# AdaLN transformer layer on one core: new order of the steps, 95 score units on row tiles, ten more unread products

## What is computed

```python
mod = (_silu(L0_c) @ L0_wmod).reshape(4, 6, 1, -1)          # sa, ca, ga, sb, cb, gb; |ga|, |gb| at least 0.25
h = _layernorm(x) * (1 + ca) + sa
x = x + ga * attention(h)      # 16 query heads summed in groups onto 4 key heads, d = 16, rope, causal softmax over 1024
h = _layernorm(x) * (1 + cb) + sb
x = x + gb * ffn(h)            # per position: h if not routed, else h' + mlp(rmsnorm(h')),
                               # h' = h + (rmsnorm(h) @ wv) @ wo, mlp = silu(a @ w_gate) * (a @ w_up) @ w_down, 704 wide
```

## Time and profile before

| | |
|---|---|
| median of 3 runs | 460.96 us |
| the profiled execution: its own time | 461.26 us |
| its span, first to last instruction | 459.5 us |
| mean granted TensorE clock | 0.996 of full |
| TensorE busy (matmuls) | 431.0 us, 94% |
| VectorE busy | 350.9 us, 76% |
| ScalarE busy | 307.9 us, 67% |
| POOL busy | 190.8 us, 42% |
| chain that ended last, by engine | TensorE 81%, VectorE 7%, ScalarE 5% |

### The profile page before, as it was taken

How to read it: one execution, slowest core, us unless ns; L and a number is a source line. 1 busy time by engine, 2 the same in 40 slices (tenths; PEclk the granted TensorE clock), 3 DMA queues, 4 the chain that set the end, 5 groups by cost and what they waited for, 6 DMA issues and landing times.

```text
span 459.5 us, 9532 instructions
## 1 busy us (share of the span) xinstructions
PE 431.0 (94%) x3320; PEld 364.0 (79%) x3320; DVE 350.9 (76%) x796; ACT 307.9 (67%) x640; POOL 190.8 (42%) x308
## 2 busy tenths in 40 slices
PE   6897879888999999999999999999999999999996
PEld 6575444776586688997858999999898698999996
DVE  4789958789988578998847889888975755588554
ACT  2398588775688886527697645667768698646441
POOL 6485546410256210424917204533244333436633
PEclk9998999999999999999999999999999999999999
DMA  6940030000001000020120000000010000000001
GB/s 192 324 152 14 1 100 0 2 1 3 0 3 34 22 1 1 2 69 1 44 71 24 2 1 24 1 26 24 2 58 3 24 23 3 25 1 24 23 25 47
DMA packets 16577, 16.05 MB, mean 35 GB/s; under 512 B 4233, under 2 KB 14926, under 8 KB 16530
## 3 DMA queue, kind: packets, MB, share of 16 engines
q1 hardware_dynamic: 16530, 15.44, 10.9%
HBM read 11.09 MB, written 4.21 MB: 33 GB/s over the span
## 4 chain that ended last, share of the span: by engine, by line
PE 81%; DVE 7%; ACT 5%; issue 3%; POOL 1%; DMA 1%; SPq 1%; ACTq 0%; DVEq 0%; POOLq 0%
PE banks L812 9%; PE banks L814 9%; PE banks L813 9%; PE banks L740 6%; PE banks L703 6%; PE banks L599 6%; PE banks L601 6%; PE banks L600 6%; PE banks L728 6%; PE banks L681 5%; DVE mxp L1185 2%; PE banks L691 2%; ACT xTc L913 1%; PE banks L795 1%; PE banks L776 1%
## 5 line engine op out<-in xcount | busy, mean ns | idle before, releaser
L812 PE MATMUL banks<-gTh,guhi 128*128 128x256 f32 x352 | 101.4, 288 | 0.1
L814 PE MATMUL banks<-gTh,gulo 128*128 128x256 f32 x352 | 98.9, 281 | 0.0
L813 PE MATMUL banks<-gTl,guhi 128*128 128x256 f32 x352 | 98.8, 281 | 0.0
L957 ACT ACTIVATE PT<-banks 128x1024 f32<-128x1024 f32 (+3 forms) x96 | 74.3, 813 | 27.7 <-PE banks L728 22.5
L812 PEld LDWEIGHTS banks<-gTh,guhi 128*128 128x128 f32 x352 | 66.4, 189 | 1.9 <-issue 1.1
L1185 DVE TENSOR_REDUCE mxp<-banks 128x2 f32<-128x1024 f32 (+3 forms) x56 | 62.1, 1142 | 6.6 <-PE banks L703 3.9
L813 PEld LDWEIGHTS banks<-gTl,guhi 128*128 128x128 f32 x352 | 66.5, 189 | 0.3
L814 PEld LDWEIGHTS banks<-gTh,gulo 128*128 128x128 f32 x352 | 66.3, 188 | 0.0
L703 PE MATMUL banks<-QKT 128*128 128x512 f32 (+3 forms) x192 | 50.3, 371 | 7.0 <-ACT QKT L935 3.4
L599 PE MATMUL banks<-wdhi,ffhi 128*128 128x256 f32 x160 | 46.1, 288 | 0.0
L728 PE MATMUL banks<-QKT 64*128 64x512 f32 (+7 forms) x192 | 44.1, 382 | 1.2 <-ACT PT L957 0.9
(11 more groups left out here) (180 smaller groups left out, 1101.0 us busy)
## 6 DMA issues: line engine op xcount, KB each, us to landing
xres<-in_L_attn_x SPq DMA_DIRECT2D x8, 512.0 KB, 4.2
out_x<-xres SPq DMA_DIRECT2D x16, 256.0 KB, 2.1
...
modB<-mod_scratch SPq DMA_DIRECT2D x4, 256.0 KB, 3.4
...
```

The source lines that it names most:

```text
L812: pe.matmul(out_, guhi[:, k, blk, :], gh, start=(m == 0 and k == 0), stop=False)
L813: pe.matmul(out_, guhi[:, k, blk, :], gl, start=False, stop=False)
L814: i = pe.matmul(out_, gulo[:, k, blk, :], gh, start=False, stop=(m == len(blocks) - 1 and k == KB - 1))
L957: act.activation(PT[:, u % 2, 2 * q:2 * q + 2, 0:CH - q0], both("prob", b, n)[:, :, 0:CH - q0], ACT.Exp, scale=float(D) ** -0.5).then_inc( ...
```

## The change

`ORDER` is replaced as a whole. It has 1450 words again, the same number of each kind; their sequence, the banks and the marks differ. Marked are now 72 `prob` and 23 `max` steps. `FILL` is keyed by batch too, and puts 3 unread products ahead of the first `max` of batch 0, 2 ahead of its first `yT`, and 5 ahead of its first `ynT`, beside the 6 ahead of the first `qkv`. In `max`, `yT` and `ynT` the wait for the bank now comes ahead of the wait for the data, with the unread products between.

The diff, with most of the two lists left out:

```diff
--- before.py
+++ after.py
@@ -42,7 +42,7 @@
 NX = 3
 WARM, WIDE = 14, CH // (2 * KB * B)
 
-FILL = {('qkv', 0): 6}
+FILL = {('max', 0, 0): 3, ('yT', 0, 0): 2, ('ynT', 0, 0): 5, ('qkv', 0, 0): 6}
 HALVES = slice(0, CH // 2), slice(CH // 2, CH)
 
 
@@ -111,65 +111,65 @@
 
 
 ORDER = """
-ldx ldx ldx ldx pzero asetw stats setw pmodc vmodc rstd1 norm1 norm1 xT4 xev qkv5 stats norm1 norm1 xT4 xev qkv4 asetb
-setb pmod amod rstd1 norm1 norm1 xT6 xev norm1 norm1 xT7 qkvb qkvb rope pprep0 afwv vkeys sthi qkv6 xev aprep pprep1
-aw1 gmod stlo qkvb qkv7 qkvb gprep stats rstd1 norm1 stack4 stack6 rope stk max4 max0 stk mxr mxr sthi stlo aprep max6
-max2 max4 stack0 mxr stack6 stk aprep mxr mxr max2 max0 max4 mxr stk mxr max2 max0 mneg mtT6 mrow max6 mxr mxr mxr ldW
-ldB ldG ldG max2 max0 max4 mxr mxr mxr max6 mxr mxr mrd prob2' aprep awd exp norm1 gprep max0 max4 prob6' max2 mxr mxr
-exp prob0' max6 prob4' exp norm1 norm1 gprep gw1 gprep gwd pmask max0 exp mxr mxr mxr pv2 prob4' prob6' pmask pv
-prob0' exp exp pmask exp prob4' exp mneg mtT3 mrow mrd ldx pmask pv pv ycopy yT2 xT3 xev xT4 wob woh ldx stats ytm
-ynT5 ynev prob2 prob0 rstd1 wol norm1 wo5 x1 rstd2 norm1 norm1 norm2 exp exp norm1 prob6' exp prob2' prob0' pv5 prob6
-exp wo2 pv exp exp prob0' exp x1 rstd2 prob6' exp stats rstd1 pv prob2' prob0' prob6' exp exp pv exp hT2 hhi prob0
...
-ytm a3 route stlo h2 h2T2 a5 qkv7 h2hi ynT3 qkvb qkvb stack0 ms2 ynev stk stack6 h2lo stk route ms2 max0 rope sthi
-max4 max6 up2 mxr mxr max0 norm1 rs2 norm1 h2 gate3 sil max4 mxr max6 mxr stlo mxr mxr stack0 stack4 stk h2 max0 fft
-max2 h2T6 stk mneg mtT7 mrow h2hi mxr mxr max4 max0 max2 norm1 mxr mxr mxr max4 wo7 max0 h2lo mxr max2 gate6 ffhi sil
-mrd prob4 x1 rstd2 exp wo6 gate7 mxr mxr max0 mxr prob4' prob2' x1 exp exp max0 mxr max4 prob2 pmask pv6 norm1 exp
-pmask mxr max0 mxr max2 prob4 exp pv prob4 exp woh mxr max0 mxr mneg pmask prob4 exp up2 prob4 exp xT3 xev norm1 norm1
-pmask rstd2 norm2 gate0 fflo fft sil pv pv mtT3 mrow norm2 sil hT1 hhi hlo ycopy ms1 rs1 up4 xT2 norm1 ffhi gate3 yT6
...
+ldx stats asetw setw rstd1 pmodc norm1 norm1 norm1 xT5 norm1 vmodc xev qkv5 stats xT7 xev vkeys rstd1 asetb pmod pzero
+norm1 setb qkv7 amod norm1 qkvb norm1 xT4 norm1 qkvb pprep0 gmod xev rope xT7 afwv qkv4 pprep1 xev qkvb sthi stlo qkv3
+aw1 stats stack4 stack0 qkvb stk rope stk max6 max2 max4 mxr sthi max0 mxr ldW aprep stlo max2 mxr stack6 gprep mxr
+max4 stk mxr stack0 mxr stk max6' mneg max4 mxr mtT1 mrow mxr max6 aprep mrd max0 ldx ldx ldG mxr max2' mxr aprep
+gprep mxr max0 max6 mxr rstd1 prob4' prob2 exp mxr max0' norm1 exp prob4 mxr gw1 max6 exp max2 mxr pmask prob0 exp wob
+max6' mxr aprep pmask mxr gprep max2' max0 awd mxr max4 pv7 mxr woh mxr prob0' prob2' exp pv exp mneg prob0' prob4 exp
+pmask exp mtT6 pmask mrow pv norm1 pv norm1 ycopy mrd ldx gprep yT1 xT6 ytm xev wol ynT4 stats ynev gwd ldW prob0
...
+norm2 exp xT4 pmask prob2 prob0 stats exp a7 rs1 exp prob2 xev prob0' pmask pv route norm1 a4 exp exp ms2 hT2 pmask
+route pv hhi norm1 pv hlo qkv0 ms2 norm1 ms1 qkvb rs2 a3 ycopy qkvb rs1 h2 xT7 rope h2 yT6 xev xT1 h2T5 h2hi qkv2 ytm
+sthi a0 xev route ynT7 ynev qkv4 stlo qkvb ms2 h2lo stack6 qkvb stack2 stk route rope stk max6 max0 mxr sthi max2 mxr
+gate6 stlo max0 mxr sil max4 mxr stack2 mxr max0 stk stack6 mxr wo4 stk max2' mneg mxr mtT5 up0 mrow x1 ms2 mrd max2'
+rs2 gate7 fft rstd1 mxr h2 h2 max4 sil max0 mxr h2T3 mxr max6' h2hi prob4' exp h2lo mxr max2 prob0 mxr max6 exp mxr
+prob2' pmask max4' exp prob0' rstd1 mxr ffhi max6 exp max2 mxr wo4 norm1 pmask max0' mxr gate7 rstd2 x1 norm1 pv6 mxr
+prob2' max4' exp pv mxr woh max0 prob2 mxr max4 exp pmask prob2' mxr exp prob0 norm1 exp up3 rstd2 sil mneg pmask up0
...
 """.split()
@@ -615,7 +615,7 @@
 
                 def fill(kind, n):
                     free(kind, n)
-                    for _ in range(FILL.get((kind, n), 0) if b == 0 else 0):
+                    for _ in range(FILL.get((kind, b, n), 0)):
                         pe.matmul(of(kind, b, n)[:, 0:P], ident[:], ident[:], start=True, stop=True)
 
                 if kind == "pmodc":
@@ -693,8 +693,8 @@
                     i.then_inc(S["stack"], 1)
                 elif kind == "max":
                     qt, k0, kn, at = MAX_UNITS[n]
+                    fill(kind, n)
                     wait("stk", qt // 2 + 1)
-                    free(kind, n)
                     o = both(kind, b, n)
                     diag = k0 + kn == (qt + 1) * P
                     for m, q in enumerate(at):
```

More of the change, by code:

```diff
@@ L139 @@
-sil up1 ffl fft max4 mxr max2 max0 wo6 max4 up7 mxr mxr mxr gate2 x1 sil ffhi fft max4 mxr up3 ffhi fflo max0 mxr
-gate2 sil fft ffl wo7 woh max4 mxr down6 sum prob0 rs1 a2 route x1 prob4 down6 sum ffhi exp exp prob0 prob4 exp rstd2
-pmask rstd2 exp fflo max2 mxr pv7 ms2 prob4' exp prob0' exp a6 max4 route ms2 pmask pmask pv prob0' prob2' exp down6
-rs2 exp pmask pv pv mxr mneg mtT2 store ldx stats sum hT3 h2 h2 h2T4 ycopy yT7 ytm mrow mrd down6 fin rstd1 store
-norm1 ynT7 hhi hlo sum fin store norm1 h2hi h2lo a5 route wol ldW ldx ldG a6 prob2 prob0 prob4 route ynev wo7 x1 norm2
@@ new lines @@
+sil xev prob6' a0 fflo exp yT3 hT4 ytm down1 ms1 route hhi prob6 route ms2 ynT3 exp down2 sum hlo ynev ms2 prob6' sum
+prob0' exp fin prob4' pv3 exp wo6 exp a2 x1 prob0' norm1 pv store exp ldG ldB rs1 prob4' prob6' norm1 exp route pv rs2
+exp prob4' prob0' rstd2 ms2 up2 exp norm1 exp a7 pv pmask route prob4' fft prob0' exp prob6' pv exp wo4 ms2 exp prob0
+rs2 x1 qkv2 h2 h2 pmask h2 up5 exp pmask h2T1 fft xT0 prob6 norm2 xev prob4' pv pv h2hi exp gate0 h2lo exp ffhi pmask
+fflo norm1 up4 sil norm1 pv qkv5 qkvb rstd2 ycopy xT1 qkvb ffhi hT2 xev xT6 fft ffl gate3 rope hhi qkv7 sil ffhi wob
@@ new lines @@
+yT4 xev qkvb up5 fflo sthi gate1 fft stlo ffhi h2 qkv5 hlo sil ytm stack2 qkvb stack0 stk gate4 rope max6 sil up2 ms1
+mxr fflo stk up5 fft max6 fft sthi max2 mxr h2T4 ffhi max0 h2hi mxr ffl max6 down5 mxr mxr stlo ynT1 max6 norm2 stack2
+down0 stk mxr sum ynev h2lo max2' stack6 sum mxr wo4 stk gate5 x1 ffhi max2' mneg sil max6 rstd2 mxr max0 fin mtT5 mxr
+up4 mrow mxr max2 fft max0 mxr store up4 mxr max6' fflo max2' gate5 ldx mrd mxr mxr max0 sil gate6 ffhi fft mxr max2
+sil max4 mxr up7 mxr max2 prob0' mxr exp wo4 down5 fflo x1 ffhi prob0' woh max2 fft down4 exp mxr ffhi pmask sum ffl
@@ new lines @@
+prob0 sum max2 exp fflo prob4' mxr pv7 exp rs1 prob0' mneg prob4' pmask exp a3 exp mtT0 route pmask mrow prob4' pv fin
+stats pv ms1 mrd a2 exp prob0 hT6 exp route down5 ms2 pmask store ms2 hhi rs2 prob2' sum prob0' exp pv rstd1 down5
+ycopy exp rs1 h2 yT7 norm1 h2 sum prob0' hlo norm1 prob2' exp fin ytm prob4' pv6 exp a1 exp prob2' route ynT0 exp h2T4
+a7 h2hi rstd2 ldG store xT5 ynev route pv xev wol prob0' prob2' exp h2lo pv ldW ldx norm2 exp prob4 prob0' exp pv exp
+prob4' prob2' exp hT7 pmask wo1 exp prob4' x1 pv ms2 pmask ms2 prob2' exp rs2 pv stats exp prob0' norm1 prob4' exp up3
@@ new lines @@
+exp pmask h2 hhi rstd1 ms1 gate0 hlo h2 norm1 a2 sil rs1 h2T5 a7 norm1 route pmask qkv1 h2hi norm1 wob ms2 fft pv
+norm2 ffhi pv xT4 up3 xev norm1 route ldB norm1 gate0 qkvb h2lo qkv7 sil ms2 fft ycopy xT0 fflo gate1 xev qkvb rope
+ffhi hT2 sil up6 ffl qkv5 fft sthi wo7 qkvb rs2 up4 hhi stlo hlo rstd2 xT5 x1 gate1 xev ffhi yT6 sil stack2 fflo h2
+qkv7 ytm h2 stk stack0 qkvb down6 stk rope ms1 max2 sthi down0 rs1 mxr sum fft ffhi max4 sum stlo h2T7 fin gate0 mxr
+h2hi max2 sil up4 mxr store h2lo ynT2 fft gate1 norm2 a5 sil fflo gate0 ynev route up7 sil ms2 wo4 fft ffhi stack2 x1
@@ new lines @@
+ffl wo6 stk a0 up5 route ffhi gate4 fft x1 max0 sil stack2 ms1 mxr up4 ms2 rs1 fflo ffhi hT5 fft max6 rstd2 hhi down0
+stk mxr rs2 hlo h2 max6 h2 sum fflo down1 mxr max4' sum max2' mneg fin a1 mxr h2T0 mtT7 mxr gate6 h2hi mrow h2lo max4
+ffhi norm2 mrd sil up7 ffl gate2 route a0 fft ms2 ms1 up3 mxr route sil ffhi up1 fft fflo ffhi ms2 max4' max6' mxr rs2
+gate0 rs1 mxr up4 sil max2 fft gate0 ffhi mxr h2 ffl h2 fflo max6' sil prob2' h2T5 exp fft rstd2 down1 mxr h2hi hT7
+sum ffhi down4 h2lo hhi norm2 prob2' prob0' sum exp up5 hlo fin exp max2' prob0' mxr gate7 exp ms1 pmask fflo max0 sil
@@ new lines @@
+a3 mxr a6 route gate0 fft ms2 route ffhi up7 sil fflo ms2 woh max4 rs2 down2 mxr rstd2 h2 h2 fft rs1 wol max6' sum hT0
+mxr h2T1 pmask max2' h2hi down5 ffhi hhi hlo max6 sum h2lo gate4 fin mxr up5 sil mxr prob2' pv0 fft ldG store store pv
+exp max4 prob6 mxr gate1 exp pmask norm2 prob6 prob4 exp a3 exp ffhi a2 route sil ldB store pmask gate6 ffl mneg up5
+sil ms1 pv fft pv route mtT7 ycopy up5 ffhi fflo mrow yT6 fft hT4 ms2 mrd gate3 ytm hhi ffhi ms2 fflo up2 sil rs2
+down0 fft ffl ffhi h2 rs1 prob2' sum prob6' exp fflo down5 ynT0 sum down1 hlo ynev fin exp a4 h2 sum prob2 route wo5
```

54 lines of the change are left out of this document (15 added, 39 removed).

## The result

| | before | after |
|---|---|---|
| median of 20 runs each, in turn on one chip | 461.77 us | 459.18 us |
| lowest to highest | 460.85 to 466.02 | 455.27 to 461.81 |
| profiled execution: its own time | 461.26 | 459.68 |
| its span | 459.5 | 458.0 |
| its mean granted clock | 0.996 | 0.985 |

The ratio of the times is 0.9925, with a 95% interval of 0.9906 to 0.9944: some 3 us faster, where 458.1 us and a gain of 2.9 us were predicted. The time is in the range. The way to it is not the predicted one, and the rest of this text is about that. Of all runs in this text one (of old_order_new_marks, 474.95 us) fell into a slower state of the chip and is left out of its median and means.

A forecast was written before the change was run, and what follows sets the result against it. TensorE bounds 115 to 440 us; before that VectorE's pace and the waits count. Marks 5.1 us less, changes of form 3.2 more, head 1.0 less: 2.9 less than 461.26, 458.4, set at 458.1 for the median; range 454.0 to 464.0.

The forecast's parts named there:

- Part 1: Behind about 131 us, 43 more marked units on TensorE, 0.14 us saved per unit of 512 columns: 5.1 us less.
- what would show it: List of signs; one: a marked unit between full products has pitch 0.33 to 0.43, products beside it 0.1 more each.
- Part 2: Behind about 131 us, TensorE switches between full array, marked units and `pv` 101 times instead of 52: 3.2 us more.
- R to C: nothing: On TensorE, going from marked units (two row tiles) to `pv` (four column tiles) costs no extra time.
- Rival A: Changes of form on TensorE are hidden and cost nothing: 454.9 us, or 454.2 with both VectorE gaps closed; chance 0.15.
- Part 3: Ahead of about 131 us, 12 more marks and 15 more changes of form count nothing, covered by VectorE's reductions.
- Part 4: Ten unread products in TensorE's waits of the first batch, 0.25 us each: no cost, at worst 2.5 us.
- Part 5: At the head, `vkeys` and `pzero` move earlier and close VectorE gaps of 0.91 and 0.82 us: 1.0 us less.
- Part 6: The rest of the order, with the same steps per engine: counted as nothing, 2 us to either side.
- B: Changes of form cost more, up to 0.20 us each, where TensorE is never idle: slower, 464.7 us; chance 0.20.
- C: At the head, a wait from `pmod` or modB makes it 1.8 us more: 460.9 us, no change; chance 0.10.
- D: A second half-clock stretch on TensorE, 3.40 us long, loses up to 1.7 us: 459.8 us; chance 0.08.

The follow-up runs named there:

- old_order_new_marks: The kernel before, its own order, banks and unread products kept, with the change's 95 marks in place of its 40: 465.86 us, ratio 1.0085.
- lone_off: The changed kernel with the marks off the 16 units that stand alone between two full-array products: 456.45 us, ratio 0.989.
- nomarks: The changed kernel with all 95 marks taken off, its order, banks and unread products kept: 461.57 us, ratio 0.9998.
- early_marks_off: The changed kernel without the 32 marks ahead of the second `mtT` of batch 1, the 63 later ones kept: 458.12 us, ratio 0.9909.
- gwd_lone: The changed kernel with `gwd` and the steps that feed it moved earlier and the 16 lone marks off: 455.62 us, ratio 0.9872.
- combined: The changed kernel with `gwd` and its feeders earlier, the 32 early marks off and the later lone marks off: 458.37 us, ratio 0.9917.

## Why the prediction was right, and where not

**The sum came out by errors that cancel, which is luck.** Before is 460.5 us at full clock and the change 455.1: 5.4 us less, twice the predicted gain. Then 6 us more at 0.50 take back 6 x 0.33 = 2 us. That leaves 3.4, the measured ratio's 461.77 x 0.0075 = 3.5. By place: the late stretch, where the prediction had 1.9 us less, gave 0.4. The start, where it had 1.0 less, gave 4.6 at full clock (second `mtT` at 131.09 with 3.4 us at 0.50, against 129.93 with 13.7).

**Part 1, marks: the term that was mis-sized, 5.1 us for what is 3.0.** The prediction read 0.33 for a marked unit from a pair and took it for every unit. The pitches show 0.197 for each group of adjacent marked units and 0.234 for each unit of 512 columns in it. Behind the cut the 20 marks of before make 10 groups and hold as many columns as 17 units of 512; the 63 of the change make 39 groups, 19 of them of a single unit, and hold as many as 54. So the marks save 37 x 0.236 - 29 x 0.197 = 3.0 us. The 0.33 to 0.43 for a lone unit stood in what would show it, while the sum used 0.33 for all.

**Part 2, changes of form: prices right beside ordinary products, the sum somewhat high.** The products behind marked ones have 0.23, those ahead 0.1 more, as forecast. "R to C: nothing" is true only because the 0.33 held the charge already: a marked group pays its 0.197 beside `pv` too. Beside transpositions an unmarked unit pays as well, so a mark costs nothing more there (lone_off). Two pairs of kernels that differ in the marks alone test the prices in the late stretch without an assumption on the order (changes of form counted in the lists, the four prices those of the prediction):

| late stretch | by the sum of the prediction | with the price of a group | measured |
|---|---|---|---|
| nomarks to the change | 5.6 less | 3.2 less | 3.6 less |
| before to old_order_new_marks | 1.3 more | 5.4 more | 3.6 more |
| before to the change | 1.9 less | 0.1 more | 0.4 less |

So the missing 1.5 us need no effect of the new order: 2.1 lie in the price of a group, which part 1 left out, and some 0.6 go the other way, in changes that cost less than 0.1. In the old order, where 37 of the marked units stand alone, the sum is 1.8 too high, so an effect of the order of 1 us is not excluded. Rival A is out by both pairs.

**Part 3, early marks: wrong.** Counted as zero because VectorE's reductions cover TensorE there. Two pairs of kernels (the change and early_marks_off, gwd_lone and combined) say 1.7 and 2.2 us at full clock. The step that failed is the one from "VectorE works without a gap from 41.93 to 55.97" to "nothing else counts before 131 us": behind 58 us VectorE is busy for only 11.84 of 17.00 us in the kernel before. Which wait the marks shorten there is open.

**Part 4, unread products: right.** No cost (455.6 without, 455.0 to 455.2 with them).

**Part 5, the head: the gain is there and hidden, and `gwd` was missed.** `stats` of batch 1 starts at 29.2 against 29.0, so the 1.0 us does not show. But the x that the second `stats` of batch 0 needs landed 1.1 us later in this trace (at 13.76 against 12.68). From that `stats` to the one of batch 1 the change takes 15.4 us and before 16.3. The traces of the new order that have no half clock there give 15.4 to 15.7, those of the old order 15.7 to 16.3: a gain of some 0.5 us, where 1.0 was forecast. The landing itself varies, from 12.7 to 13.6 in the old order and from 13.2 to 13.8 in the new. The 13 reductions end at 57.9 and not at 55, nor are they unbroken: they lie in a stretch at half clock and wait for TensorE. Without it, in nomarks, they end at 55.8, against 56.0. And of `gwd` the prediction said that it would end some 10 us later and looked only at who waits for its result, the loads of x; `norm2` did not wait for modB at all. It ended 16 us later, at 66.40, and what counted was what ran beside it. The term that was missing is 3.1 us on VectorE and 3.14 on TensorE; with `gwd` moved away `ynT` comes 1.5 to 1.85 us sooner in spite of the new waits, and the kernel is some 0.9 us faster at full clock, which is within the scatter.

**Part 6, the rest of the order: the largest miss of a term.** Taken as 0 with 2 us to either side, on the ground that both orders issue the same steps ahead of the cut. nomarks shows 3.6 us there, head and unread products included, up to 1.1 of it by the clock, and with the 3.1 us block of `gwd` inside. The number of steps says nothing of the waits between them: before, TensorE waited 1.53 us for hbuf (L998), 1.08 for QKT (L935) and 0.77 for xTc (L913) between 75 and 96 us; after, 20.58 of 21.00 us are work. Each of these waits is one row in the trace of before, and the prediction weighed none of them.

**The rivals.** A is excluded by nomarks and old_order_new_marks, though its gain of 6.1 us is near the 5.4 at full clock: that gain was made in the first 130 us, not where A had it. B is out by the sign, but its point, that leaving and entering the marked form cost more than the sum had, is what the runs show, 1.5 us of it and not the 2.9 that would have made the kernel slower. C is excluded by the absence of its waits. D happened, 6.9 us and not 3.4 of it, at 66 us. It was priced at half its length at most; the slope says a third. Why it happened is open. It is not the order alone (nomarks has 4.8 us at 0.50 over its runs), nor less work on TensorE ahead of the second `mtT`, where its idle time fell from 22.4 us to 17.3. 32 early marks go with 7 us more in one pair of kernels, and 24 of them with 1.3 less, which is within the scatter, in the other.
